# A Mamba block's front written out batch by batch, with its residual moved into the scan stage

## The chip, the cores and the metric

The kernel runs on one core of one Trainium2 chip. The metric is the time of one launch on the device in microseconds (us): the median of several runs. All data is float32 unless a tile is said to be something else.

## The reference, cut to what matters

The input is x, 8 batches of 512 tokens of 128 features. Four blocks follow each other, each added to its input: a Mamba block, a mixture of experts, an attention block, the same mixture of experts again. The change touches the Mamba block alone:

```
xl    = layernorm(x)                                  # (x - mean) * rstd
xn    = xl * rsqrt(mean(xl * xl) + eps) * norm_w
x_s,z = split(xn @ in_proj_w.T)                       # 256 channels each
u     = silu(causal_conv4(x_s) + conv_b)
dt,B,C= split(u @ x_proj_w.T)                         # 8, 16, 16
delta = softplus(dt @ dt_proj_w.T + dt_proj_b)
h_t   = exp(delta * A) * h_(t-1) + delta * u * B_t    # 16 states per channel
y     = (sum over states of h_t * C_t + u * D) * silu(z)
x     = x + (y @ out_proj_w.T + xl)                   # xl is the block's own residual
```

The last line is x * (1 + rstd) - mean * rstd + y @ out_proj_w.T, and both kernels compute it in that form.

## The kernel before, in words

The program is written by hand for each engine, and engines meet at semaphores. `setup` loads x into the tile `x_tok` (128 tokens by 32 groups by 128 features; four groups are one batch) and computes `mean`, `rstd` and `r12` (the product of both scales) for every token. `mamba` then runs two stages with a barrier between them: `mamba_front` and `mamba_scan`. The rest of the launch (the experts, attention, the experts) is the same code in both kernels.

**The front** makes, for each of 8 batches, `delta`, `du` = delta * u, `u`, `zs` = silu(z) and the turned B (tile `b_T`), all but the last kept in the large tile `arena`, and stores the rows of C to memory. A batch takes this way through the engines:

- VectorE (DVE in the rows) makes the normalised rows `xn_tok` (`normed`, L422, four instructions of 128x128); TensorE (PE) turns them (`turn`, L348); ScalarE (ACT) copies them out (`x_out`, L534); PE projects to x_s (L366) and to z (L360).
- The convolution: ACT makes the first tap (L540), DVE the other three taps for two channel halves, six instructions (`conved`, L449, of which one input is in PSUM and one in SBUF). ACT applies silu (`u_out`, L547; `gates` for z, L553).
- PE projects u (`x_proj`, L374), ACT copies (`xd_out`, L564), PE projects dt (L383). ACT takes the absolute value (L570), loads another function table, and makes exp and ln (`logs`, L575 and L578).
- softplus is max(v, 0) + log1p(exp(-|v|)), and log1p is made exact in pieces: DVE `lows` (L477, an SBUF tile to an SBUF tile, 1024 elements a partition); GpSimd (POOL) subtracts and adds (L606, L609); DVE `bounds` (L482) takes the minimum; DVE `deltas` (L461, two instructions, from PSUM) makes max(v, 0); POOL adds the two (L612, delta) and multiplies by u (L616, du). L471 on DVE copies the turned B.
- The residual: DVE multiplies `x_tok` by 1 + rstd and subtracts mean * rstd (`residual`, L436, four instructions of 128x128, SBUF to SBUF).

The order on each engine is the written order. For DVE, after a start written out for batches 0 and 1, a loop of B - 2 = 6 turns (L492 to L501) does in turn b: `normed(b + 2)`, `conved(b + 1)`, `lows(b)`, `deltas_and_b(b)`, `residual(b + 2)`, `bounds(b)`. PE, ACT and POOL have loops that fit this one. In POOL's loop a batch's four operations stand together: subtract, add, delta, du. For the last batch DVE itself does those operations (L511 to L518). A loop's turn computes addresses in registers, and each engine gives an increment more after some waits (`k.passed`).

**The scan stage** has 8 batches of 16 states, that is 128 steps. In a step ACT scales du by B (L722, four instructions) and makes exp(delta * A) (`d_a`, L730, two instructions), PE turns the product into PSUM (L820, or L817 for four of the states), DVE scans (L936), POOL multiplies by C (L681), PE adds up (L837). Each batch's output is made during the next batch's steps: in step 5 and 6 the gated rows are turned and copied (L953), in step 7 PE runs `project` (L856: for four groups of tokens two matmuls with `w_out` each) and DVE runs `add` (L949: one instruction over 512 elements, PSUM and x_tok into x_tok). In step 8 and 9 DVE makes the statistics of the next block's layernorm (L1069, L1074) and copies the next batch's du (L957), and in step 10 ACT makes the scale of these statistics (L1142) between its own scaling and its exps. At the start of the stage PE turns du of batch 0 into two banks (L794), ACT copies them (L708), and only then can ACT begin with L722.

## Time and profile before

| what | value |
|---|---|
| median of 3 runs | 1303.31 us (1302.11 to 1303.85) |
| the profiled execution, its own time | 1301.48 us |
| its span in the trace | 1299.7 us |
| front, first instruction of DVE to the end of its last | 24.20 to 150.90 us |
| scan stage begins | 152.03 us |
| TensorE busy, share of the span | 1067.4 us, 82% |
| VectorE | 928.6 us, 71% |
| ScalarE | 869.2 us, 67% |
| GpSimd | 540.6 us, 42% |

The spans of the profile are of one execution, whose own time is 1.8 us more than its span and 1.83 us less than the median of the runs. The shares are means over stages of different kinds. In the front and in the scan stage the engines stand otherwise than over the whole: what a change there is worth is read from stretches of the trace.

### The profile page before, as it was taken

The numbers are of one execution on the slowest core, as the hardware profiler recorded it, in microseconds if no ns is written. First come the engines' busy times: TensorE is split into PE (matmuls) and PEld (weight loads), VectorE is DVE, ScalarE is ACT, GpSimd is POOL, SyncE is SP. The second block draws the span as 40 slices with busy tenths as digits, with TensorE's granted clock in tenths as the row PEclk, the third lists the DMA queues.
The fourth block names the chain that finished last, engine by engine and source line by source line (L and its number), as shares of the span: only waits on it lengthen the run. The fifth ranks groups of instructions, "written<-read, shape, count | busy, mean of one in ns | idle before, by whom it ended". The sixth has DMA issues, their size and how long they took to land. (4 is left out here: it accounts for less than half of the span.)

```text
span 1299.7 us, 25092 instructions
## 1 busy us (share of the span) xinstructions
PE 1067.4 (82%) x7486; PEld 753.5 (58%) x7486; DVE 928.6 (71%) x2003; ACT 869.2 (67%) x1835; POOL 540.6 (42%) x367
## 2 busy tenths in 40 slices
PE   1677499988989888638966999999999999981797
PEld 1333278878878788518963454545454544541796
DVE  5899499889889889435644677757685867763564
ACT  1777699999999999216743756656675666660574
POOL 0367488899999999713440001010101011011344
PEclk9888699999999999878987999998999999995899
DMA  3000133223463453113321000000000000001331
GB/s 87 2 3 2 34 96 95 96 87 109 149 192 107 149 161 107 40 54 93 93 68 58 1 2 18 1 18 1 17 1 18 1 17 13 5 17 54 88 92 46
DMA packets 50631, 74.40 MB, mean 57 GB/s; under 512 B 7351, under 2 KB 28604, under 8 KB 50528
## 3 DMA queue, kind: packets, MB, share of 16 engines
q1 hardware_dynamic: 41504, 51.09, 13.5%
q0 software_dynamic: 5568, 12.66, 2.7%
q10 hardware_dynamic: 3456, 9.46, 2.3%
q8 instruction: 41, 0.67, 0.2%
q14 instruction: 62, 0.51, 0.1%
HBM read 57.86 MB, written 16.24 MB: 57 GB/s over the span
## 5 line engine op out<-in xcount | busy, mean ns | idle before, releaser
L936 DVE TENSOR_TENSOR_SCAN h<-d_a,p_dbu 128x1024 f32<-128x1024 f32 x128 | 290.1, 2279 | 37.0 <-ACT d_a L730 30.9
L681 POOL TENSOR_TENSOR h<-h,c_rep 128x1024 f32<-128x1024 f32 x128 | 299.4, 2364 | 25.2 <-DVE h L936 23.8
L1859 ACT ACTIVATE at_probs<-at_scores,at_min 128x512 f32<-128x512 f32 x256 | 184.1, 722 | 135.9 <-DVE at_min L1969 87.5
L1969 DVE CUSTOM_DVE_ANT_0 at_scores<-at_p_scores,arena 128x512 f32<-128x512 f32 x256 | 174.4, 684 | 89.5 <-PE at_p_scores L1735 51.2
L1217 POOL TENSOR_SCALAR r_row<-r_row 128x4 f32<-128x4 f32 x16 | 3.7, 231 | 476.3 <-DVEq L1130 476.3
L730 ACT ACTIVATE d_a<-arena,a_exp 128x511 f32<-128x511 f32 x256 | 169.1, 708 | 0.6 <-DVE h L936 0.5
L1742 PEld LDWEIGHTS at_p_probs_T<-ident,at_probs 128*128 128x128 f32 x1024 | 112.7, 142 | 93.7 <-issue 71.1
L1742 PE MATMUL at_p_probs_T<-ident,at_probs 128*128 128x128 f32 x1024 | 159.1, 283 | 6.4 <-ACT at_probs L1859 6.0
L722 ACT ACTIVATE b_du_T<-arena,b_T 128x256 f32<-128x256 f32 x384 | 162.5, 494 | 0.1
L1735 PE MATMUL at_p_scores<-arena,at_q_T 64*128 64x512 f32 x512 | 157.7, 643 | 5.5 <-DVE at_min L1969 3.8
L837 PE MATMUL p_y_T<-ident,h 128*128 128x128 f32 x1024 | 135.0, 275 | 7.4 <-POOL h L681 7.3
L837 PEld LDWEIGHTS p_y_T<-ident,h 128*128 128x128 f32 x1024 | 116.9, 142 | 9.9 <-POOL h L681 9.9
L820 PE MATMUL p_dbu<-ident,b_du_T 128*128 128x128 f32 x768 | 113.9, 284 | 5.0 <-ACT b_du_T L722 3.5
L1978 DVE COPY at_probs_T<-at_p_probs_T 128x512 f32<-128x512 f32 x128 | 88.2, 689 | 24.7 <-PE at_p_probs_T L1742 24.5
L820 PEld LDWEIGHTS p_dbu<-ident,b_du_T 128*128 128x128 f32 x768 | 86.5, 143 | 21.5 <-ACT b_du_T L722 9.1
L1827 ACT ACTIVATE at_probs_T<-at_p_probs_T 128x512 f32<-128x512 f32 x128 | 75.3, 588 | 26.6 <-PE at_p_probs_T L1742 24.1
L1416 PE MATMUL f_p_y<-f_w_cur,f_h_T 128*128 128x128 f32 x624 | 84.1, 278 | 7.0 <-issue 3.9
L1439 ACT ACTIVATE f_h_T<-f_p_h,f_w_cur 128x128 f32<-128x128 f32 x312 | 88.8, 376 | 1.4 <-PE f_p_h L1404 1.1
L1404 PE MATMUL f_p_h<-f_xg_T,f_w_cur 128*128 128x128 f32 x624 | 87.5, 286 | 0.9 <-issue 0.5
L1431 ACT ACTIVATE f_xg_T<-f_p_xg 128x128 f32<-128x128 f32 x78 | 21.7, 279 | 98.4 <-PE f_p_xg L1397 72.3
L1416 PEld LDWEIGHTS f_p_y<-f_w_cur,f_h_T 128*128 128x128 f32 x624 | 76.6, 193 | 8.9 <-issue 7.5
L1763 PE MATMUL at_p_o_T<-at_probs_T,arena 128*32 128x256 f32 x1024 | 80.0, 397 | 0.7 <-issue 0.7
(223 smaller groups left out, 1692.8 us busy)
## 6 DMA issues: line engine op xcount, KB each, us to landing
c_rep<-c_rows SPq DMA_DIRECT2D x128, 256.0 KB, 3.3
f_row<-expert_rows SPq DMA_DIRECT2D x78, 129.0 KB
arena<-in_w_all ACTq DMA_DIRECT2D x8, 578.0 KB
arena<-bias_by_distance ACTq DMA_DIRECT2D x8, 448.0 KB
x_tok<-in_x SPq DMA_DIRECT2D x4, 512.0 KB, 5.4
x_tok<-x_between SPq DMA_DIRECT2D x8, 256.0 KB, 2.8
expert_rows<-f_pad SPq DMA_DIRECT2D x10, 129.0 KB, 2.7
expert_rows<-f_pad ACTq DMA_DIRECT2D x8, 129.0 KB, 2.8
```

The lines of the kernel that those rows point to most:

```text
L681: nc.gpsimd.tensor_tensor(h[:, n % HS, :, :], h[:, n % HS, :, :], cc, ALU.mult).then_inc(prod_done, 1)
L722: nc.scalar.activation(b_du[:, s % SR, j, 0:width], src, ACT.Copy, scale=bT[:, one(b), j, s:s + 1].squeeze(1)).then_inc(scaled, 1)
L730: nc.scalar.activation(da[:, s % 2, ch, 1:], delta[:, one(b), ch, 1:].squeeze(1), ACT.Exp, scale=a_exp[:, ch, s:s + 1]).then_inc(da_ready, 1)
L820: mm = nc.tensor.transpose(dst, b_du[:, s % SR, j, ch * P:(ch + 1) * P], k.ident[:])
L837: mm = nc.tensor.matmul(p_yT[:, j, ch * P:(ch + 1) * P], h[:, n % HS, ch, j * P:(j + 1) * P], k.ident[:], is_transpose=SUM_BY_TRANSPOSE, s ...
L936: nc.vector.tensor_tensor_scan(h[:, n % HS, :, :].rearrange("p c t -> p (c t)"), da[:, s % 2, :, :].rearrange("p c t -> p (c t)"), p_dbu[: ...
L1416: mm = nc.tensor.matmul(py[:, r % YR, 0:D], ht[:, r % R, f, :], w_cur[:, r % R, FF + f * D:FF + (f + 1) * D], start=f == 0, stop=f == FC - 1)
L1439: ins = nc.scalar.activation(ht[:, r % R, f, :], ph[:, r % R, f, :], ACT.Gelu, bias=w_cur[:, r % R, 2 * FF + f:2 * FF + f + 1])
L1735: nc.tensor.matmul(psc[:, n % SCB, :], qT[par][half, hd // 2, it * P:(it + 1) * P], kT[par][half, hd // 2, :], start=True, stop=True).then ...
L1742: mm = nc.tensor.transpose(ppt[:, s % 2, j * P:(j + 1) * P], pr[:, s % 2, j * P:(j + 1) * P], k.ident[:])
L1859: nc.scalar.activation(pr[:, s % 2, :], sc[:, s % 2, :], ACT.Exp, scale=-1.0, bias=mn[:, s % 2:s % 2 + 1]).then_inc(probs_ready, 1)
L1969: V.tensor_tensor_reduce(sc[:, s % 2, :], psc[:, s % SCB, :], band[:, hd, w0:w0 + T], 1.0, 3.0e38, ALU.add, ALU.min, mn[:, s % 2:s % 2 + 1 ...
```

## The change

In the front, the loops of all engines are written out. A helper `each` runs i from -3 to 7 and calls every part with its own batch i + ahead. That gives five kinds of turn: three in which the pipeline fills, the full ones, and those in which first the normalised rows and then the convolution have run out. On DVE a turn is now `normed(i+3)`, `conved(i+1)`, `positive(i)`, `bounds(i-1)`, `take_b(i)`, `lows(i)`; on POOL `delta_du(i-1)`, `log_sums(i)`. `bounds` writes to a tile of its own, `delta_pos` has two buffers. `residual` is gone from the front.

In the scan stage, DVE's `add` is now four instructions of 128x128 that compute x * (1 + rstd) + p_x, and PE's `project` has one more matmul for each of the four groups, which puts -mean * rstd into the same PSUM bank before the others: its stationary operand is the turned table of shifts (32 partitions by 128 tokens), its moving operand one column of the identity, repeated 128 times. At the stage's start DVE makes the two tables, PE turns one, and ACT copies it ahead of its copies of du. In both `project` and `through_d` nothing else changes in order.

```diff
@@ mamba_front, each engine's turns @@
+        def each(*parts):
+
+            for i in range(-3, B):
+                for ahead, part in parts:
+                    if 0 <= i + ahead < B:
+                        part(i + ahead)
...
@@ tensor @@
-            with pe.Fori(0, B - 2) as b:
-                turn(b + 2)
-                in_proj(b + 2, z=False)
-                x_proj(b + 1)
-                dt_proj(b + 1)
-                in_proj(b + 2, z=True)
+            each((0, dt_proj), (2, project_in), (1, x_proj), (3, turn))
...
@@ vector @@
-            def residual(b):
-                dve.wait_ge(xn_ready, b + 1)
-                chn.wait()
-                for j in range(TPB):
-
-                    g = b * TPB + j
-                    xg = k.x[:, one(g), :].squeeze(1)
-                    chn.step(nc.vector.tensor_scalar(xg, xg, rone[:, one(g)], mr[:, one(g)],
-                                                     ALU.mult, ALU.subtract))
...
             def lows(b):
                 dve.wait_ge(e_ready, b + 1)
-                dve.wait_ge(delta_done, 1 + b)
+                after(dve, log1p_ready, b)
                 nc.vector.tensor_scalar(low[:], ex[:], 1.0, 1.0, ALU.add, ALU.subtract).then_inc(low_ready, 1)
...
                 dve.wait_ge(log_sum_ready, b + 1)
-                nc.vector.tensor_tensor(lg[:], low[:], ex[:], ALU.min).then_inc(log1p_ready, 1)
-
-            normed(0)
-            residual(0)
-            conved(0)
-            normed(1)
-            residual(1)
-
-            def turn(b, conv_next=True, norm_next=True):
-                if norm_next:
-                    normed(b + 2)
-                if conv_next:
-                    conved(b + 1)
-                lows(b)
-                deltas_and_b(b)
-                if norm_next:
-                    residual(b + 2)
-                bounds(b)
-
-            with dve.Fori(0, B - 2) as b:
-                chn.begin(b, 11)
-                turn(b)
...
+                after(dve, delta_done, b)
+                nc.vector.tensor_tensor(lm[:], low[:], ex[:], ALU.min).then_inc(log1p_ready, 1)
+
+            each((3, normed), (1, conved), (0, positive), (-1, bounds), (0, take_b), (0, lows))
...
@@ scalar @@
-            with act.Fori(0, B - 2) as b:
-                first_tap(b + 1)
-                logs(b)
-                x_out(b + 2)
-                u_out(b + 1)
-                gates(b + 1)
-                xd_out(b + 1)
...
+            each((1, first_tap), (0, xd_out), (2, x_out), (1, gates), (0, absolute), (1, u_out), (0, logs))
...
@@ gpsimd @@
-            with pool.Fori(0, B - 1) as b:
...
+            each((-1, delta_du), (0, log_sums))
...
@@ mamba_scan @@
+            act.wait_ge(shift_turned, 1)
+            nc.scalar.activation(shiftT[:], p_yT[0:NT, 0, 0:P], ACT.Identity).then_inc(shiftT_ready, 1)
             for half, bank in enumerate((p_x, p_small)):
                 act.wait_ge(du_turned, half + 1)
...
             def project(b):
                 pe.wait_ge(gT_ready, NC * b + NC)
                 for j in range(TPB):
+                    g = b * TPB + j
+                    nc.tensor.matmul(p_x[:, j * P:(j + 1) * P], shiftT[:], k.ident[0:NT, g:g + 1].to_broadcast([NT, P]),
+                                     start=True, stop=False)
                     for ch in range(NC):
-                        mm = nc.tensor.matmul(p_x[:, j * P:(j + 1) * P], u[:, one(b), ch, j * P:(j + 1) * P].squeeze(1),
-                                              w_out[:, ch, :], start=ch == 0, stop=ch == NC - 1)
+                        mm = nc.tensor.matmul(p_x[:, j * P:(j + 1) * P], u[:, b, ch, j * P:(j + 1) * P],
+                                              w_out[:, ch, :], start=False, stop=ch == NC - 1)
...
             turn_du(0, 1, p_small)
+            pe.wait_ge(shift_ready, 1)
+            nc.tensor.transpose(p_yT[0:NT, 0, 0:P], shift[:], k.ident[:]).then_inc(shift_turned, 1)
             pe.wait_ge(diag_ready, 1)
+            pe.wait_ge(shiftT_ready, 1)
...
             def add(b):
                 dve.wait_ge(projected, b + 1)
-                xb = k.x[:, bass.ds(b * TPB, TPB), :].rearrange("p g d -> p (g d)")
-                nc.vector.tensor_tensor(xb, p_x[:], xb, ALU.add).then_inc(added, 1)
+                for j in range(TPB):
+                    g = b * TPB + j
+                    xg = k.x[:, g, :]
+                    nc.vector.scalar_tensor_tensor(out=xg, in0=xg, scalar=one_plus[:, g:g + 1],
+                                                   in1=p_x[:, j * P:(j + 1) * P], op0=ALU.mult,
+                                                   op1=ALU.add).then_inc(added, 1)
```

In the order of VectorE's instructions, this is a turn of the front before (the loop; rows of address work, which repeat, are left out):

```order
L422 TENSOR_SCALAR xn_tok<-x_tok,mean,r 128x128
...
L449 SCALAR_TENSOR_TENSOR conv<-p_xz,vec,conv 128x511
...
L449 SCALAR_TENSOR_TENSOR conv<-p_xz,vec,conv 128x509
L477 TENSOR_SCALAR delta_low<-delta_e 128x1024
...
L461 TENSOR_SCALAR delta_pos<-p_dt,vec 128x512
...
L471 COPY b_T<-p_xdbc 128x64
...
L436 TENSOR_SCALAR x_tok<-x_tok,one_plus_rstd,mean_rstd 128x128
L482 TENSOR_TENSOR delta_ln<-delta_low,delta_e 128x1024
```

And this is a full turn after the change, from the `bounds` of one turn to that of the next:

```order
L460 TENSOR_TENSOR delta_log1p<-delta_low,delta_e 128x1024
L446 COPY b_T<-p_xdbc 128x64
L452 TENSOR_SCALAR delta_low<-delta_e 128x1024
L414 TENSOR_SCALAR xn_tok<-x_tok,mean,r 128x128 x4
L428 SCALAR_TENSOR_TENSOR conv<-p_xz,vec,conv 128x511 x2
L428 SCALAR_TENSOR_TENSOR conv<-p_xz,vec,conv 128x510 x2
L428 SCALAR_TENSOR_TENSOR conv<-p_xz,vec,conv 128x509 x2
L441 TENSOR_SCALAR delta_pos<-p_dt,vec 128x512 x2
L460 TENSOR_TENSOR delta_log1p<-delta_low,delta_e 128x1024
```

`lows` (L477, now L452) stood behind the convolution and ahead of the residual; now it stands right behind `bounds` and ahead of the normalised rows (L414).

On GpSimd, the operations of the written-out front come in this order (before, the loop had them as L606, L609, L612, L616, with address work ahead of L612 and L616):

```order
L541 TENSOR_TENSOR delta_low<-delta_e,delta_low 128x1024
L544 TENSOR_TENSOR delta_low<-delta_low,delta_ln 128x1024
L532 TENSOR_TENSOR arena<-delta_log1p,delta_pos 128x1024
L535 TENSOR_TENSOR arena<-arena 128x1024
L541 TENSOR_TENSOR delta_low<-delta_e,delta_low 128x1024
```

The order of the four is the same; the address work between them is gone.

On TensorE, around `project` in the scan stage, after the change:

```order
L772 MATMUL p_y_T<-ident,h 128x128 x8
L791 MATMUL p_r_x<-ident,shift_T 128x128
L794 MATMUL p_r_x<-w_out,arena 128x128 x2
L791 MATMUL p_r_x<-ident,shift_T 128x128
L794 MATMUL p_r_x<-w_out,arena 128x128 x2
L791 MATMUL p_r_x<-ident,shift_T 128x128
L794 MATMUL p_r_x<-w_out,arena 128x128 x2
```

Before, `L856 MATMUL p_r_x<-w_out,arena 128x128 x8` stood there alone; the four L791 are new, and the step's next products (L820 before, L755 now) come behind them.

## Rows read from the trace of the kernel before

**Rows 1.** Busy time by engine: a stretch of the front, and one of the scan stage.
```profile
core 0: us, PE busy (x) PEld busy (x) DVE busy (x) ACT busy (x) POOL busy (x), PEclk, DMA share, GB/s
104.00:118.20 14.20, 10.87 (x28) 5.32 (x28) 14.20 (x20) 10.49 (x15) 9.52 (x4) 0.82 0.01 2
450.00:500.00 50.00, 44.16 (x378) 40.87 (x376) 45.12 (x49) 48.17 (x109) 47.54 (x27) 1.00 0.51 154
```

**Rows 2.** Timeline of VectorE, one turn: start, duration, engine, line, operation, tiles.
```profile
103.90 0.67 DVE L477 TENSOR_SCALAR delta_low<-delta_e 128x1024 f32<-128x1024 f32 x1
104.50 1.39 DVE L461 TENSOR_SCALAR delta_pos<-p_dt,vec 128x512 f32<-128x512 f32 x2
105.95 4.07 DVE L436 TENSOR_SCALAR x_tok<-x_tok,one_plus_rstd,mean_rstd  x4
109.95 1.21 DVE L482 TENSOR_TENSOR delta_ln<-delta_low,delta_e 128x1024 f32<-128x1024 f32 x1
111.08 3.14 DVE L422 TENSOR_SCALAR xn_tok<-x_tok,mean,r 128x128 f32 x4
114.15 4.01 DVE L449 SCALAR_TENSOR_TENSOR conv<-p_xz,vec,conv 128x511 f32<-128x511 f32 x6
118.09 0.68 DVE L477 TENSOR_SCALAR delta_low<-delta_e 128x1024 f32<-128x1024 f32 x1
```

**Rows 3.** Timeline of GpSimd in the same turn.
```profile
104.66 2.35 POOL L606 TENSOR_TENSOR delta_low<-delta_e,delta_low 128x1024 f32<-128x1024 f32 x1 [2.21 <-DVE delta_low L477]
107.09 2.34 POOL L609 TENSOR_TENSOR delta_low<-delta_low,delta_ln 128x1024 f32<-128x1024 f32 x1
111.43 2.46 POOL L612 TENSOR_TENSOR arena<-delta_ln,delta_pos 128x1024 f32 x1 [2.00 <-DVE delta_ln L482]
114.27 2.36 POOL L616 TENSOR_TENSOR arena<-arena  x1 [0.38 <-POOL arena L612]
```

**Rows 4.** Single durations in ns by line: least, median, most; first and last start.
```profile
L436 DVE TENSOR_SCALAR x_tok<-x_tok,one_plus_rstd,mean_rstd x32: 333/343/2511, 25.5 to 123.9; - x24, 128x128 f32<-128x128 f32 x8
L477 DVE TENSOR_SCALAR delta_low<-delta_e x8: 672/676/1712, 47.0 to 142.3; 128x1024 f32<-128x1024 f32 x8
L461 DVE TENSOR_SCALAR delta_pos<-p_dt,vec x16: 730/734/743, 47.6 to 143.9; 128x512 f32<-128x512 f32 x16
```

**Rows 5.** Timeline of VectorE: the front's start, first batch, last loop batch and end.
```profile
24.39 1.10 DVE L422 TENSOR_SCALAR xn_tok<-x_tok,mean,r 128x128 f32<-128x128 f32 x4
46.97 0.69 DVE L477 TENSOR_SCALAR delta_low<-delta_e 128x1024 f32<-128x1024 f32 x1 [0.62 <-ACT delta_e L575]
53.04 1.21 DVE L482 TENSOR_TENSOR delta_ln<-delta_low,delta_e 128x1024 f32<-128x1024 f32 x1
136.16 1.23 DVE L482 TENSOR_TENSOR delta_ln<-delta_low,delta_e 128x1024 f32<-128x1024 f32 x1 [3.44 <-POOL delta_low L609]
149.67 1.23 DVE L518 TENSOR_TENSOR arena<-arena 128x1024 f32<-128x1024 f32 x1
```

**Rows 6.** Timeline of ScalarE at the scan stage's start.
```profile
154.20 0.59 ACT L708 ACTIVATE arena<-p_r_small 128x512 f32<-128x512 f32 x1
154.91 1.70 ACT L722 ACTIVATE b_du_T<-arena,b_T 128x256 f32<-128x256 f32 x4
```

**Rows 7.** Timeline in the scan stage around `project` and `add` of one batch.
```profile
267.49 2.05 PE L856 MATMUL p_r_x<-w_out,arena 128*128 128x128 f32 x16 [0.37 <-DVE arena L953]
269.38 1.04 PE L820 MATMUL p_dbu<-ident,b_du_T 128*128 128x128 f32 x8
269.58 0.69 DVE L949 TENSOR_TENSOR x_tok<-p_r_x,x_tok 128x512 f32<-128x512 f32 x1
270.51 2.29 DVE L936 TENSOR_TENSOR_SCAN h<-d_a,p_dbu 128x1024 f32<-128x1024 f32 x1 [0.24 <-PE p_dbu L820]
274.01 0.30 ACT L1142 ACTIVATE r_lnv<-r_mv,r_eps 128x4 f32<-128x4 f32 x1 [0.93 <-issue]
```

**Rows 8.** Timeline of TensorE: `project` of the last batch.
```profile
542.69 3.60 PE L856 MATMUL p_r_x<-w_out,arena 128*128 128x128 f32 x16 [0.78 <-DVE arena L953]
```

More of the change, by code:

```diff
@@ L346, in turn @@
                 pe.wait_ge(xn_ready, b + 1)
+                after(pe, xnT_ready, b)
                 for j in range(TPB):
@@ new lines, in project_z, with project_in @@
+            def project_z(b):
+                pe.wait_ge(xnT_ready, b + 1)
+                after(pe, z_taken, b * NC)
+                for j in range(TPB):
+                    at = j % 2 * DI
+                    mm = nc.tensor.matmul(pz[:, NC + j // 2, at:at + DI], xnT[:, j * P:(j + 1) * P], w_in[:, DI:],
+                                          start=True, stop=True)
+                    if j % 2:
+                        mm.then_inc(z_half_ready, 1)
+            def project_in(b):
+                if b == 0:
+                    project_x(b)
+                    project_z(b)
+                else:
+                    project_z(b)
+                    project_x(b)
@@ L369, in x_proj @@
             def x_proj(b):
-                pe.wait_ge(xd_ready, 1 + b)
-                pe.wait_ge(bT_ready, 1 + b)
+                after(pe, xd_ready, b)
+                after(pe, bT_ready, b)
                 for ch in range(NC):
                     pe.wait_ge(u_ready, b * NC + ch + 1)
-                    mm = nc.tensor.matmul(pxd[:], w_x[:, ch, :], u[:, one(b), ch, :].squeeze(1),
-                                          start=ch == 0, stop=ch == NC - 1)
+                    mm = nc.tensor.matmul(pxd[:], w_x[:, ch, :], u[:, b, ch, :], start=ch == 0, stop=ch == NC - 1)
@@ L455, in conved, with positive, take_b @@
                             ins.then_inc(conv_ready, 1)
-            def deltas(b, ch):
-                dve.wait_ge(delta_done, 1 + b)
-                dve.wait_ge(abs_ready, 1 + b * NC + ch + 1)
-                nc.vector.tensor_scalar(mpos[:, ch, :], pdt[:, ch, :], dt_b(ch), 0.0,
-                                        ALU.add, ALU.max).then_inc(pos_ready, 1)
-            def deltas_and_b(b):
-                deltas(b, 0)
-                deltas(b, 1)
+            def positive(b):
+                after(dve, delta_done, b - 1)
+                for ch in range(NC):
+                    dve.wait_ge(abs_ready, b * NC + ch + 1)
+                    nc.vector.tensor_scalar(mpos[:, b % 2, ch, :], pdt[:, ch, :], dt_b(ch), 0.0,
+                                            ALU.add, ALU.max).then_inc(pos_ready, 1)
+            def take_b(b):
                 dve.wait_ge(b_turned, b + 1)
-                k.passed(dve)
-                nc.vector.tensor_copy(bT[:, one(b), :, :].squeeze(1).rearrange("p j s -> p (j s)"),
+                nc.vector.tensor_copy(bT[:, b, :, :].rearrange("p j s -> p (j s)"),
                                       pxd[:, 0:TPB * NS]).then_inc(bT_ready, 1)
@@ L513, in _ @@
             chn.link(nc.vector.tensor_tensor(low[:], low[:], lg[:], ALU.add))
             chn.link(nc.vector.tensor_tensor(lg[:], low[:], ex[:], ALU.min))
-            dve.wait_ge(pos_ready, 1 + B * NC)
-            chn.link(nc.vector.tensor_tensor(delta[:, last, :, :], lg[:], mpos[:], ALU.add))
+            dve.wait_ge(pos_ready, B * NC)
+            chn.link(nc.vector.tensor_tensor(delta[:, last, :, :], lg[:], mpos[:, last % 2, :, :], ALU.add))
             dve.wait_ge(u_ready, B * NC)
             chn.link(nc.vector.tensor_tensor(du[:, last, :, :], delta[:, last, :, :], u[:, last, :, :], ALU.mult))
-            chn.wait()
@@ L593, in _, with delta_du @@
-            first_tap(B - 1)
-            logs(B - 2)
-            u_out(B - 1)
-            gates(B - 1)
-            xd_out(B - 1)
-            logs(B - 1)
+            each((1, first_tap), (0, xd_out), (2, x_out), (1, gates), (0, absolute), (1, u_out), (0, logs))
         @block.gpsimd
         def _(pool):
-            k.from_one(pool, delta_done)
-            with pool.Fori(0, B - 1) as b:
-                db = delta[:, one(b), :, :].squeeze(1)
-                pool.wait_ge(low_ready, b + 2)
+            def delta_du(b):
+                pool.wait_ge(log1p_ready, b + 1)
+                pool.wait_ge(pos_ready, b * NC + NC)
+                nc.gpsimd.tensor_tensor(delta[:, b, :, :], lm[:], mpos[:, b % 2, :, :], ALU.add).then_inc(delta_done, 1)
+                pool.wait_ge(delta_done, b + 1)
+                pool.wait_ge(u_ready, b * NC + NC)
+                nc.gpsimd.tensor_tensor(du[:, b, :, :], delta[:, b, :, :], u[:, b, :, :], ALU.mult).then_inc(du_done, 1)
```

177 lines of the change are left out of this document (68 added, 109 removed).

## The prediction

> **What bounds the kernel now.** I read the busy time by stretch first, then the timeline of one turn of the front on VectorE and on GpSimd, then the single durations of a few lines, and last the timeline of the scan stage around `project`. The front bounds itself on VectorE: of a stretch of 14.20 us it is busy for 14.20, TensorE for 10.87, ScalarE for 10.49, GpSimd for 9.52 [rows 1]. The turn's length stands in the starts of `lows`, 103.90 and 118.09: 14.19 us [rows 2]. But VectorE is not at work in all of it. The four residual instructions take 4.07 us and the four normalised rows 3.14 [rows 2], while four of the same form take 1.10 at the front's start, where GpSimd does nothing [rows 5]. The difference is held time. A residual instruction has a median of 343 ns and a most of 2511 [rows 4], and the long ones end with a GpSimd operation: the stretch of L436, 105.95 to 110.02, is the rest of L606 (until 107.01), all of L609 (107.09 to 109.43), and two free instructions [rows 2, 3]. So a VectorE instruction that goes from SBUF to SBUF in this form waits until the running GpSimd operation ends; in the gap of 0.08 us between two of them exactly one gets through. `deltas`, which reads PSUM, runs beside L606 with no hold (730 to 743 ns) [rows 3, 4], and so does the convolution beside L616.
>
> In the scan stage ScalarE is busy 48.17 of 50 us [rows 1]. Of the idle rest one piece recurs: in step 10 it waits 0.93 us for VectorE's statistics before L1142 [rows 7]. From step 7 to there the path is PE and VectorE: `project` ends at 269.54, PE's next products L820 at 270.42, and VectorE's scan waits 0.24 for them, with `add` done at 270.27, just before [rows 7]. A delay there reaches ScalarE, which has nothing to make it up with.
>
> **The change, part by part.**
>
> *The full turn of the front.* The residual's 4.07 us go. That alone would leave 10.1 us of VectorE, but the order decides who is held. Now `lows` follows `bounds` at once, so GpSimd gets all its four operations in one row: delta and du of batch i-1, subtract and add of batch i. The normalised rows stand right behind `lows`, so they meet these operations: one gets through at each boundary, and the last at about the end of the add. Only then come the convolution, max(v, 0) and `bounds`, which nothing overlaps on GpSimd. From one `bounds` to the next:
> - `bounds` 1.13 (109.95 to 111.08) [rows 2], and about 0.1 until GpSimd starts;
> - GpSimd's 2.35 + 2.35 + 2.35 + 2.34, with three gaps of 0.08: 9.63 [rows 3] (L612 and L616 at the plain 2.35, since their 0.38 of gap goes with the address work);
> - `lows`: it is issued while delta runs, held, and then keeps GpSimd's du off. Its own 0.68 less the overlap is 0.55;
> - the last normalised row 0.26 ((1.10 - 0.33) / 3) [rows 4, 5], the convolution 3.94 (114.15 to 118.09), max(v, 0) 1.32 (1.39 less 0.07 of overlap) [rows 2].
>
> Together 16.9 us, against 14.2. Between bounds 0 and bounds 3 there are three such turns. In the next three the normalised rows have run out; the convolution then lies beside GpSimd, which becomes the bound: 1.21 + 0.1 + 9.63 + 0.55 = 11.5. Six turns: 3 x 16.9 + 3 x 11.5 = 85.2, against 83.1 (53.04 to 136.16) [rows 5]: **+2.1**.
>
> *The fill.* VectorE now makes three batches of rows before the first convolution, and the third waits until PE has turned the second, behind both projections; PE puts both projections of batch 1 ahead of `x_proj(0)`, and ScalarE puts `gates` and `u_out` of batch 1 ahead of the first exp. I put the convolution of batch 0 3.2 us later and the rest of the chain to `lows(0)` even, so that starts at 50.2 instead of 46.97 [rows 5]. From there to the first `bounds`: 0.68 + 0.08 + 2.35 + 0.08 + 2.34 (held rows), 0.6 for the last two, 3.94 + 1.32: 11.4, against 6.07 now [rows 2, 3, 5]. Fill: 3.2 + 5.3 = **+8.5**. I am least sure of the 3.2: from 0 (PE and ScalarE have slack while the pipeline fills) to 5.
>
> *The end.* From the last `bounds` to the front's end there are 14.7 us now (136.16 to 150.90) [rows 5]. After: 1.2 + 0.1 + 2.35 (delta) + 0.55 (`lows`) + 2.35 (du) + five closing operations at 1.25 = 12.8, **-1.9**. This takes it that the first closing operation, which reads two SBUF tiles, is held by du. No such operation stands beside a running GpSimd one in the trace: the bounds are 0 (L461, not held) and 2.35 (L477, held up to 1712 ns) [rows 4]. I take the upper, since its sources are both in SBUF like L477's. The Trainium skill (page "SBUF — State Buffer", section "Who interferes with whom") says that a tensor_tensor with both inputs in SBUF contends with GpSimd's reads; by it the sum stays, without it it would be about 2 lower. No run here shows it yet. The two small tables leave the front: -0.2.
>
> Front: 2.1 + 8.5 - 1.9 - 0.2 = **+8.5**.
>
> *The scan stage's start.* ScalarE's copies of du now wait behind PE's third transpose and the table's copy. Its second copy starts at 154.20, and the first scaling at 154.91 [rows 6]; what comes between PE's second group and the first copy now is a small transpose and a small copy, some 0.25 each, two hand-overs, and the first copy itself that moves behind them: **+0.8** (0.3 to 1.2).
>
> *Each batch's project and add.* Four more matmuls of 128 columns. Eight take 16 records in 2.05 us, with the next products 1.89 after the start [rows 7], so four cost 0.95 (the least would be half, if a matmul of 32 rows were cheaper; no row shows that). `add` becomes four of 128x128, for which I take the 1.10 of rows 5 (the bounds are the 0.69 that one takes now and four at L449's 0.67). PE: products end 0.95 later. VectorE: add starts at 270.5, ends at 271.6, and the scan starts there, against 270.51: 1.15. Nothing between there and ScalarE's wait in step 10 makes it up. Seven batches: 7 x 1.15 = **+8.0**. The last batch's project runs at 3.60 / 16 = 0.225 a record [rows 8], with VectorE waiting for it: 8 x 0.21 + 0.4 = **+2.1**.
>
> **Sum:** 8.5 + 0.8 + 8.0 + 2.1 = 19.4 us. The profiled execution would be 1301.5 + 19.4 = 1320.9, the median, 1.8 above it, 1303.3 + 19.4 = **1322.7**.
>
> **The rivals.**
> - *The scan's additions lie in ScalarE's shadow.* For it: VectorE is busy 45 of 50 us, so it has slack somewhere; against it: the 0.24 and 0.93 of rows 7 are on the very path. Then only the last batch's 2.1 and the start's 0.8 remain: 1303.3 + 11.4 = 1314.7. Chance 0.12.
> - *More rows get through a boundary.* For it: at L616's gap of 0.38 a free instruction did get through; if the gaps stay wide, the rows are done by the end of the subtract, and each held turn is 2.4 shorter, the fill too: 1322.7 - 4 x 2.4 = 1313.1. Against it: the gap without address work is 0.08 [rows 3]. Chance 0.12.
> - *Faster: the rows are not held at all in the new order*, because VectorE comes first to what the two share, or because the hold belonged to the residual's write of x_tok. Then GpSimd's 11.0 (11.5 less the 0.55) bounds every turn. `bounds(0)` would come at 50.2 + 7.0 (VectorE's own work) = 57.2, the last at 123.2, the end some 9.3 later at 132.5: the front ends 18.4 earlier, and the launch takes 1303.3 - 18.4 + 10.9 = 1295.8. It decides once the rows of a turn take under 1.5 us. Against it: xn_tok itself took 3.14 in rows 2. Chance 0.08.
> - *Longer still:* TensorE's granted clock, 0.82 of full in a turn now [rows 1], falls with longer idle stretches and stretches the fill's chain: up to 1330. Chance 0.06.
>
> The forecast keeps 0.62. **The range** is 1310 to 1330: it takes in the first two rivals, the fill's 0 to 5 and the closing hold, and leaves out the third. About 0.2% (2.6 us) is what a measurement of this kernel can tell from no change. Faster by more than that 0.08, within it 0.04, slower 0.88.
>
> **What would show it.** In the profile after: L414 with 24 of its rows near 0.34 us or less and some ten of over 2; a full turn of 16.9 and late ones of 11.5 by the starts of L460; GpSimd's four operations back to back; the first L460 near 61 or 62; L791 as 8 records a batch; `add` of some 1.1 us and VectorE's next scan 1.15 later than project allows now; ScalarE's wait before its step 10 scale near 2.1. I am wrong if the rows L414 take about 1.1 a batch in full turns, or if the stretch from project to L1142 keeps its length of 6.5 us (267.49 to 274.01) [rows 7].

## The result, and the profile after

The changed kernel takes 1321.13 us (median of 4 runs, 1319.66 to 1322.63), the kernel before 1303.58 on the same chip. The ratio is 1.0137, with an interval of 1.0113 to 1.0161: slower by 17.5 us, where 1322.7 was forecast. The profiled execution took 1321.48 us, with a span of 1319.5 against 1299.7. Busy time hardly moves: TensorE 1086.8 us against 1067.4, VectorE 926.7 against 928.6.

The place of the time comes from the same instructions in both traces. "How much later" is the start after less the start before.

| instruction | before | after | later by |
|---|---|---|---|
| `lows(0)` | 46.97 | 52.68 | 5.71 |
| first `bounds` | 53.04 | 64.00 | 10.96 |
| last closing operation of the front | 149.67 | 158.82 | 9.15 |
| scan of batch 0, step 1 | 162.07 | 171.72 | 9.65 |
| scan of batch 3, step 0 | 295.25 | 307.23 | 11.98 |
| scan of batch 7, step 0 | 483.23 | 501.26 | 18.03 |
| scan of batch 7, step 15 | 527.95 | 547.18 | 19.23 |
| last `r_dest` of the scan stage | 562.37 | 583.39 | 21.02 |

(`r_dest`, the table of each token's place in the next block, is made once a batch; the last one ends the scan stage's own work.) Behind the scan stage 1.2 us come back (the span is 19.8 longer), but that is scatter: the stretch from the last `r_dest` to the end, whose code is the same everywhere, takes 734.9 to 739.1 us in all kernels here but one. So the loss lies in the front (9 us) and in the scan stage (12 us).

**The front.** First VectorE, then GpSimd, in one full turn: start, duration, engine, line, operation. Rows 2 and 3 show the same turn before.

```profile
64.00 1.21 DVE L460 TENSOR_TENSOR delta_log1p<-delta_low,delta_e 128x1024 f32<-128x1024 f32 x1
66.39 1.81 DVE L452 TENSOR_SCALAR delta_low<-delta_e 128x1024 f32<-128x1024 f32 x1 [1.05 <-ACT delta_e L519]
68.12 7.35 DVE L414 TENSOR_SCALAR xn_tok<-x_tok,mean,r 128x128 f32<-128x128 f32 x4
75.39 4.02 DVE L428 SCALAR_TENSOR_TENSOR conv<-p_xz,vec,conv 128x511 f32<-128x511 f32 x6
79.33 1.40 DVE L441 TENSOR_SCALAR delta_pos<-p_dt,vec 128x512 f32<-128x512 f32 x2
80.65 1.21 DVE L460 TENSOR_TENSOR delta_log1p<-delta_low,delta_e 128x1024 f32<-128x1024 f32 x1
```

```profile
65.29 2.36 POOL L532 TENSOR_TENSOR arena<-delta_log1p,delta_pos 128x1024 f32<-128x1024 f32 x1 [7.06 <-DVE delta_log1p L460]
67.72 2.68 POOL L535 TENSOR_TENSOR arena<-arena 128x1024 f32<-128x1024 f32 x1
70.37 2.34 POOL L541 TENSOR_TENSOR delta_low<-delta_e,delta_low 128x1024 f32<-128x1024 f32 x1
72.78 2.35 POOL L544 TENSOR_TENSOR delta_low<-delta_low,delta_ln 128x1024 f32<-128x1024 f32 x1
```

The turn is 16.65 us (64.00 to 80.65) against 14.19 [rows 2]. Four normalised rows last 7.35 us, from the middle of du to the end of the add; the convolution begins at 75.39, when GpSimd is through (75.13) and does nothing for the rest of the turn. Of the 32 rows 21 take 0.33 to 0.35 us, and 11 take 1.74 to 2.51.

**The scan stage**, around `project` and `add` of one batch (rows 7 of before): TensorE, VectorE, ScalarE.

```profile
279.50 0.48 PE L791 MATMUL p_r_x<-ident,shift_T 32*128 32x128 f32 x2 [0.37 <-DVE arena L903]
279.91 0.71 PE L794 MATMUL p_r_x<-w_out,arena 128*128 128x128 f32 x4
280.56 0.48 PE L791 MATMUL p_r_x<-ident,shift_T 32*128 32x128 f32 x2
...
283.08 0.71 PE L794 MATMUL p_r_x<-w_out,arena 128*128 128x128 f32 x4
283.63 1.04 PE L755 MATMUL p_dbu<-ident,b_du_T 128*128 128x128 f32 x8
```

```profile
279.36 2.28 DVE L882 TENSOR_TENSOR_SCAN h<-d_a,p_dbu 128x1024 f32<-128x1024 f32 x1
283.83 1.12 DVE L897 SCALAR_TENSOR_TENSOR x_tok<-x_tok,one_plus_rstd,p_r_x 128x128 f32<-128x128 f32 x4 [2.19 <-PE p_r_x L794]
284.87 2.28 DVE L882 TENSOR_TENSOR_SCAN h<-d_a,p_dbu 128x1024 f32<-128x1024 f32 x1
```

```profile
284.70 1.71 ACT L657 ACTIVATE b_du_T<-arena,b_T 128x256 f32<-128x256 f32 x4 [1.22 <-PE p_dbu L755]
288.36 0.30 ACT L1092 ACTIVATE r_lnv<-r_mv,r_eps 128x4 f32<-128x4 f32 x1 [1.95 <-DVE r_mv L1024]
299.66 0.58 ACT L1098 ACTIVATE arena<-p_r_x 128x512 f32<-128x512 f32 x1
```

`project` takes 4.29 us (279.50 to 283.79), not 2.05. VectorE waits 2.19 for it, and its scans of steps 7 and 8 start 5.51 us apart. ScalarE's wait in step 10 has grown from 0.93 to 1.95. But L1098 in step 13 waits for nothing, where the same copy in the trace of before waited 1.17 us (0.83 in later batches):

```profile
286.57 0.60 ACT L1148 ACTIVATE arena<-p_r_x 128x512 f32<-128x512 f32 x1 [1.17 <-PE p_r_x L1168]
```

So a batch loses in step 7 and gets a part back in steps 13 to 15. Taken over whole batches (scan 0 to scan 0 of the next), after is 2.35 us longer than before in batch 1, where nothing comes back, no longer in batch 2, 1.84 in batch 3 and 1.4 in batches 4 to 6. The experiments take both places apart.

### The profile page after: what moved, and what is told of

Same layout as the page of the kernel before. It is cut to its first block and busy times, and to the rows that moved or that the text cites. A ratio compares the mean times of both kernels' runs of the same rounds, so it can differ in the third digit from the quotient of the medians.

```text
span 1319.5 us, 24770 instructions
## 1 busy us (share of the span) xinstructions
PE 1086.8 (82%) x7551; PEld 763.4 (58%) x7551; DVE 926.7 (70%) x1995; ACT 868.4 (66%) x1835; POOL 542.6 (41%) x367
## 5 line engine op out<-in xcount | busy, mean ns | idle before, releaser
L755 PE MATMUL p_dbu<-ident,b_du_T 128*128 128x128 f32 x768 | 118.7, 284 | 6.4 <-ACT b_du_T L657 4.0
L755 PEld LDWEIGHTS p_dbu<-ident,b_du_T 128*128 128x128 f32 x768 | 84.0, 142 | 31.8 <-ACT b_du_T L657 14.1
```

What stands on the lines that cost most here:

```text
L755: mm = nc.tensor.transpose(dst, b_du[:, s % SR, j, ch * P:(ch + 1) * P], k.ident[:])
```

## The experiments

All times are medians, and ratios are to the kernel before, run beside each. Those medians of before lie between 1302.44 and 1305.58 us, so kernels of different sets are better compared by their ratios. "Step 7" is the distance of VectorE's scans 7 and 8 of a batch, "late" that from scan 13 to scan 0 of the next batch, both from VectorE's timeline; the trace of before has 3.16 and 10.2, that of after 5.50 and 9.04 (batches 3 to 6).

### The scan's additions apart

**scan_plain**: no shift matmul, the plain add, no tables.

```diff
-                    nc.tensor.matmul(p_x[:, j * P:(j + 1) * P], shiftT[:], k.ident[0:NT, g:g + 1].to_broadcast([NT, P]),
-                                     start=True, stop=False)
...
-                    nc.vector.scalar_tensor_tensor(out=xg, in0=xg, scalar=one_plus[:, g:g + 1],
-                                                   in1=p_x[:, j * P:(j + 1) * P], op0=ALU.mult,
...
+                nc.vector.tensor_tensor(xb, p_x[:], xb, ALU.add).then_inc(added, 1)
```

> The changed kernel with the scan stage as before: project without the shift matmuls, one plain add of 512 elements a batch, no tables. The residual's share of the normalised input is left out altogether, so the time is that of the front's change alone. Theory (front +9.1 us, the rest of the +17.5 from the scan's additions): 1309 to 1311 us. Rival (the additions lie in ScalarE's shadow and the front costs it all): 1318 to 1321.

**adds_only**: the first part of this diff alone (no shift matmuls), without the shift's table as well. **shift_only**: the other part alone (one plain add in place of the four).

> The changed kernel with the four adds but without the shift matmuls and their table (the term -mean*rstd is left out). Theory (a delay under the 1.2 us that the late steps regain costs nothing but in the last batch): within 1 us of scan_plain, about 1310.5. Rival (the adds' 0.43 us a batch adds up): 8 x 0.43 = 3.4 above scan_plain, 1313.5 to 1314.

> The changed kernel with the four shift matmuls a batch kept but the four adds back to one plain add (the factor 1 + rstd on the old row is left out). Theory (project's extra 2.2 us is what costs, and of each batch's delay about 1.2 us is regained in the late steps): 7 x (2.0 - 1.2) above scan_plain and about 2 for the last batch, 1317 to 1319. Rival (nothing is regained, the delays add up plainly): 7 x 2.0 + 2, 1325 or the changed kernel's own time; rival (the four adds are the cost): near scan_plain's 1310.

| kernel | us | ratio, interval | step 7 | late | last `r_dest` later than before |
|---|---|---|---|---|---|
| scan_plain | 1309.71 | 1.0040, 1.0021 to 1.0058 | 3.16 | 10.2 | 7.73 |
| adds_only | 1310.81 | 1.0035, 1.0020 to 1.0050 | 3.27 | 10.1 to 10.2 | 8.97 |
| shift_only | 1326.45 | 1.0161, 1.0129 to 1.0192 | 5.39 | 9.04 | 19.09 |
| after | 1321.13 | 1.0137, 1.0113 to 1.0161 | 5.50 | 9.04 | 21.02 |

scan_plain's ratio puts the front's change at 2.7 to 7.6 us, where its trace has 7.7 by the last `r_dest` and 9.1 by the first scans; the profiled execution of before is one of the faster ones. The four adds cost nothing that a run can tell: their 0.43 us (1.12 less 0.69) lie beside TensorE's products, and step 7 grows by 0.11. From scan 0,1 (batch 0, step 1) to scan 7,15 adds_only takes 365.79 us and scan_plain 365.78. The shift matmuls are 2.23 us of step 7, 1.2 of which the late steps return from batch 3 on. They can't return more than that: at 9.04 ScalarE waits for nothing in them. In batch 1 they are at 9.04 in the kernel before too, and return nothing. So the rival "lies in the shadow" held for the adds and fell for the matmuls.

shift_only was expected at 1317 to 1319 and took 1326.45. Its theory had the scan stage 7.6 us longer than scan_plain's; by the last `r_dest` it is 11.4 (581.46 less 570.10), of which 8.7 lie between scan 0,1 and scan 7,15 where 5.6 were expected: batch 1 returned nothing. It is 1.9 us ahead of after there. The rest of its launch takes 740.8 us (1322.3 less 581.46) against 736.1. It leaves a factor out, so its later stages work on other values; but scan_plain leaves out more, and its rest takes 737.0. The cause of these 4 us is open.

### Why four small matmuls cost 2.2 us

**shift_wide** (one matmul of 512 columns ahead of the others) and **shift_first** (all four of 128 columns ahead, each with its weight load), each against after:

```diff
+                rows = k.ident[0:NT, b * TPB:(b + 1) * TPB].unsqueeze(2).to_broadcast([NT, TPB, P])
+                nc.tensor.matmul(p_x[:].rearrange("p (j i) -> p j i", i=P), shiftT[:], rows,
+                                 start=True, stop=False, skip_group_check=True)
```

```diff
                     nc.tensor.matmul(p_x[:, j * P:(j + 1) * P], shiftT[:], k.ident[0:NT, g:g + 1].to_broadcast([NT, P]),
-                                     start=True, stop=False)
+                                     start=j == 0, stop=False, skip_group_check=True)
+                for j in range(TPB):
                     for ch in range(NC):
```

> The changed kernel, computing the same, with one shift matmul of 512 columns ahead of the eight others in place of four of 128 between them. Theory (the cost is the change between 32-row and 128-row matmuls, some 0.3 us a time): project takes 2.9 to 3.1 us in place of 4.29, each batch gains 1.2, the time is 1321 - 7 x 1.2 - 1 = 1311 to 1314. Rival (a column of a 32-row matmul is dear in itself, 0.56 us for 128): project stays at 4.2 to 4.4 and the time within 2 us of the changed kernel's.

> The changed kernel, computing the same, with the four shift matmuls of 128 columns together ahead of the eight others, each with its own weight load. It parts two readings of shift_wide. Theory (a change between 32-row and 128-row matmuls is what is dear): project 3.0 to 3.3 us, VectorE's step from scan 7 to scan 8 at 4.3 to 4.6 us, 1313 to 1316 us. Rival (each separate matmul of 32 rows with its own weight load is dear, wherever it stands): project 4.1 to 4.3, the step 5.4 to 5.5, 1319 to 1322.

TensorE in shift_wide, and then in shift_first:

```profile
277.50 1.12 PE L790 MATMUL p_r_x<-ident,shift_T 32*128 32x512 f32 x2 [0.37 <-DVE arena L904]
278.56 2.05 PE L794 MATMUL p_r_x<-w_out,arena 128*128 128x128 f32 x16
```

```profile
277.92 1.15 PE L791 MATMUL p_r_x<-ident,shift_T 32*128 32x128 f32 x8 [0.37 <-DVE arena L905]
279.00 2.05 PE L795 MATMUL p_r_x<-w_out,arena 128*128 128x128 f32 x16
```

Both have the same work as after and take 3.1 us for `project` in place of 4.29. Step 7 is 4.32 and 4.35, late 9.1; the times are 1314.88 (ratio 1.0065, 1.0040 to 1.0089) and 1315.17 (1.0091, 1.0067 to 1.0115). shift_wide is just above the 1311 to 1314 expected, shift_first within its range. Separate weight loads are not it (1.15 against 1.12). What is dear is that matmuls of 32 rows and of 128 rows (32*128 and 128*128 in the lines) alternate: (4.29 less 3.13) / 4, about 0.3 us a group. Grouping leaves one change of kind where after has seven, so a change costs (4.29 less 3.13) / 6, about 0.19 us. The weight loads (PEld) in after's `project` show where:

```profile
279.50 0.29 PEld L791 LDWEIGHTS p_r_x<-ident,shift_T 32*128 32x128 f32 x2 [0.61 <-DVE arena L903]
279.91 0.52 PEld L794 LDWEIGHTS p_r_x<-w_out,arena 128*128 128x128 f32 x4
```

Behind a change the load starts together with its matmul (279.91 both), 0.20 us after the start of the matmul before, and the second matmul 0.21 after the first. Within a kind the load starts 0.11 ahead of its matmul, and matmuls follow each other at 0.11.

Is it the number of rows, or that the small matmul's moving operand is one column repeated? The trace of before answers, since attention changes between 64 and 128 rows with ordinary operands:

```profile
709.41 1.04 PE L1742 MATMUL at_p_probs_T<-ident,at_probs 128*128 128x128 f32 x8
710.37 1.13 PE L1735 MATMUL at_p_scores<-arena,at_q_T 64*128 64x512 f32 x4
```

At such a change, 91 times in this trace, the first 64-row matmul starts 0.20 us after the last 128-row one, while the 128-row ones follow each other at 0.11. So the repeated column isn't needed, and the delay at a change could be read before the prediction.
The Trainium skill (page "TensorE: Matmul & The Clock Gate", section "LDWEIGHTS (loading the stationary operand)") says that a 32x128 load takes as long as a 128x128 one. The trace agrees: a load of 32 rows takes 0.18 to 0.19 us, one of 128 rows 0.19. By that rule the four cost what four large ones do; grouped they cost about that (0.27 each, against 0.24 for a w_out matmul), but alternating they cost 0.56, of which the rule says nothing.

### The order of the front

**rows_late** moves the rows in VectorE's turn; **rows_act** leaves the place and gives them to ScalarE.

```diff
-            each((3, normed), (1, conved), (0, positive), (-1, bounds), (0, take_b), (0, lows))
+            each((1, conved), (0, positive), (3, normed), (-1, bounds), (0, take_b), (0, lows))
```

```diff
+                    ins = nc.scalar.activation(xn[:, j, :], k.x[:, g, :], ACT.Identity, scale=k.r12[:, g:g + 1],
+                                               bias=nmr[:, g:g + 1])
...
-            each((1, first_tap), (0, xd_out), (2, x_out), (1, gates), (0, absolute), (1, u_out), (0, logs))
+            each((3, normed), (1, first_tap), (0, xd_out), (2, x_out), (1, gates), (0, absolute), (1, u_out), (0, logs))
```

> The changed kernel with the normalised rows of a turn behind the convolution and max(v, 0), just ahead of bounds. Theory (the rows are dear because GpSimd's four operations run behind bounds and lows, and a row gets through only between two): they take 1.1 to 1.5 us, a full turn some 12.3 us in place of 16.65, three turns 13 less, and the fill 4 to 9 less: 1299 to 1305 us. Rival (the order in VectorE's turn doesn't matter, the turn is bound by the chain through TensorE and ScalarE): a full turn stays over 15.5 and the time above 1317.

> The changed kernel with the normalised rows made on ScalarE (scale r12, bias -mean*r12) at the start of its turn; VectorE's order is the same less the rows. Theory (the hold is on VectorE alone): no row takes over 0.4 us, a full turn comes to 11.2 to 12.5 us, the last convolution no longer waits for GpSimd, 1298 to 1304 us. Rival (any engine's read of x beside GpSimd is held, or ScalarE's four more operations bound the turn): rows of 1 us and more or a turn over 14, 1310 or more.

rows_late, VectorE's turn:

```profile
70.63 1.21 DVE L460 TENSOR_TENSOR delta_log1p<-delta_low,delta_e 128x1024 f32<-128x1024 f32 x1
...
74.79 4.04 DVE L428 SCALAR_TENSOR_TENSOR conv<-p_xz,vec,conv 128x511 f32<-128x511 f32 x6
79.57 1.41 DVE L441 TENSOR_SCALAR delta_pos<-p_dt,vec 128x512 f32<-128x512 f32 x2 [0.74 <-ACT delta_abs L512]
80.89 1.77 DVE L414 TENSOR_SCALAR xn_tok<-x_tok,mean,r 128x128 f32<-128x128 f32 x4
82.59 1.21 DVE L460 TENSOR_TENSOR delta_log1p<-delta_low,delta_e 128x1024 f32<-128x1024 f32 x1
```

One line moved, a full turn of 11.96 us in place of 16.65, and 1302.28 us (ratio 0.9995, 0.9977 to 1.0013). The time is in the 1299 to 1305 expected, though four rows take 1.77 us and not 1.1 to 1.5. The front's last operation starts at 139.41, 19.4 earlier than after's. The convolution, which isn't held (0.73 to 0.75 us an instruction, as in after and before), now lies beside GpSimd's operations, and the rows meet only the end of the last one. The first `bounds` comes at 58.68, 5.3 earlier, 2.5 of it for the held rows behind `lows(0)`, and 2.8 because `lows(0)` comes at 49.87 and not 52.68.

These 2.8 us are of two kinds. After and the five kernels of the two sections above have the same front, and their `lows(0)` lies between 51.70 and 52.72. TensorE's granted clock from 34 to 44 us is 0.83 in after and 1.00 in shift_wide, whose `lows(0)` is at 51.70, and 1.00 in rows_late too. So 1.0 us goes by the clock and 1.8 is the rows' place. VectorE at the second convolution, in after and then in rows_late:

```profile
44.56 1.11 DVE L414 TENSOR_SCALAR xn_tok<-x_tok,mean,r 128x128 f32<-128x128 f32 x4 [5.74 <-PE p_xT L355]
45.59 4.02 DVE L428 SCALAR_TENSOR_TENSOR conv<-p_xz,vec,conv 128x511 f32<-128x511 f32 x6
```

```profile
41.37 4.17 DVE L428 SCALAR_TENSOR_TENSOR conv<-p_xz,vec,conv 128x511 f32<-128x511 f32 x6 [4.67 <-ACT conv L488]
```

In after the fourth batch of rows stands ahead of the second convolution and waits for TensorE's `turn` (L355), which stands behind `x_proj(0)`. ScalarE's `u_out(1)` waits for that convolution, and the first exp stands behind `u_out(1)`. The third batch of rows ahead of the first convolution moves that by 4 us (34.80 in after, 35.27 in shift_wide, 30.60 in rows_late), but `x_proj(0)` comes at 41.23 in shift_wide and 41.15 in rows_late all the same.

In rows_act no row is held: the 32 take 477 to 493 ns, those beside GpSimd's operations too. But ScalarE had no room:

```profile
78.92 4.04 DVE L424 SCALAR_TENSOR_TENSOR conv<-p_xz,vec,conv 128x511 f32<-128x511 f32 x6 [2.95 <-ACT conv L493]
85.01 1.21 DVE L456 TENSOR_TENSOR delta_log1p<-delta_low,delta_e 128x1024 f32<-128x1024 f32 x1
```

```profile
76.57 1.65 ACT L479 ACTIVATE xn_tok<-x_tok,minus_mean_r,r 128x128 f32<-128x128 f32 x4 [1.02 <-PE p_xT L357]
78.12 1.42 ACT L493 ACTIVATE conv<-p_xz,vec 128x512 f32<-128x512 f32 x2
```

The rows wait there for TensorE and push the first tap back, on which VectorE now waits 2.95. A turn is 13.25 (71.76 to 85.01), the first `bounds` 7.8 later than in after, and the time 1320.78 (ratio 1.0129, 1.0093 to 1.0166), not the 1298 to 1304 expected. ScalarE's rows aren't held, but the place was wrong again.

**logs_first**, on rows_late: for batch 0 only, ScalarE does exp and ln ahead of gates and u of batch 1.

```diff
+                if i == 0:
+                    behind = ((0, absolute), (0, logs), (1, gates), (1, u_out))
```

> rows_late with one turn of ScalarE's order changed: the exp and ln of batch 0 ahead of the gates and u of batch 1. Theory (the fill's later lows(0) is ScalarE's order: gates and u of batch 1, 2.24 us, stand ahead of the first exp): the exp starts some 2.2 earlier, lows(0) at 48.2 to 48.6 where VectorE's own order then holds it, in place of 49.87. Rival (the exp waits for TensorE's dt): lows(0) stays within 0.3 of 49.87. The launch's time moves by less than 2 us either way.

`lows(0)` stays at 49.65, as the rival says, since the exp waited for TensorE's dt. But this run doesn't clear ScalarE's order: its granted clock from 34 to 44 us is 0.83, against 1.00 in rows_late, and `x_proj(0)` comes 0.82 later (41.97 against 41.15). From there the exp starts 6.59 us on, against 7.63 in rows_late, so the order is worth about 1.0 us, which the clock hides. The launch moved by far more than expected: the gates of batch 1 came at 52.01, the projection behind them at 53.24, and the first `bounds` at 66.22 in place of 58.68. 1312.73 us (1.0059, 1.0039 to 1.0079); 3.6 us of it are two falls of the clock in `project` (the last section). So of the 2.9 us by which rows_late's `lows(0)` is later than before's, about 1.0 is ScalarE's order, by this reading. The rest stands with TensorE, which starts `x_proj(0)` at 41.15 in rows_late and at 36.81 before; a kernel with TensorE's old order was not run.

**fold_loop**: the kernel before, its loop less the residual, with the scan's part of the change.

```diff
-                if norm_next:
-                    residual(b + 2)
```

> The kernel before with the scan's part of the change alone: the front's loop as before less its residual, the shift matmuls and the four adds in the scan stage. Theory (in the old order bounds follows GpSimd's subtract and add, which start with lows, so the residual's 4.07 us lay almost wholly beside them): a full turn goes from 14.19 to 13.6 or 13.8 us, the front ends 2 to 4 earlier, the scan's additions cost some 11.5: 1311 to 1314 us. Rival (the 4.07 us come off each turn): a turn of 10.1 to 10.6, 1303.5 - 24 + 11.5 = 1291.

VectorE, one turn:

```profile
108.06 1.23 DVE L467 TENSOR_TENSOR delta_ln<-delta_low,delta_e 128x1024 f32<-128x1024 f32 x1 [3.43 <-POOL delta_low L590]
109.20 3.14 DVE L417 TENSOR_SCALAR xn_tok<-x_tok,mean,r 128x128 f32 x4
...
121.77 1.22 DVE L467 TENSOR_TENSOR delta_ln<-delta_low,delta_e 128x1024 f32<-128x1024 f32 x1 [3.43 <-POOL delta_low L590]
```

A turn of 13.71, with 3.43 us of waiting where the residual stood: its 4.07 us were worth 0.5. 1314.41 us (1.0067, 1.0038 to 1.0095), just above the 1311 to 1314 expected; two falls of the clock in `project` make its scan stage some 3.4 us longer than after's. The last `bounds` of the loop comes 2.4 earlier than before (133.79 against 136.16), but the front's last operation only 0.8, less than the 2 to 4 expected. So the fold had next to nothing to gain in the old order.

### Versions that beat both

**best1**: rows_late's order, the residual on ScalarE in the front, the scan stage as before. **best2**: rows_late with shift_wide. **best3**: rows_late's order, the scan stage as before, the residual on VectorE where it idles beside an idle GpSimd, and the first normalised rows no longer behind the wait for the weights. Its residual:

```diff
+            def residual_in_fill(b):
+                if b < 3:
+                    residual(b)
...
+            for g in range(3 * TPB, NT):
+                chn.step(nc.vector.tensor_scalar(k.x[:, g, :], k.x[:, g, :], one_plus[:, g:g + 1], mr[:, g:g + 1],
+                                                 ALU.mult, ALU.subtract))
```

> Meant to beat both kernels: the changed kernel's written-out front with the normalised rows just ahead of bounds, the residual done in the front by ScalarE (scale 1 + rstd, bias -mean*rstd, four operations at the end of its turn), and the scan stage as before with one plain add. Theory: scan as before, so 1310.5 less the 17 to 22 of the new order, 1289 to 1295 us. Rival (ScalarE becomes the front's bound): a full turn over 13.5, 1297 or more; rival (the order doesn't matter): 1308 or more.

> rows_late with shift_wide's project: the normalised rows ahead of bounds, one shift matmul of 512 columns, the four adds. Theory (the two parts add up, -19 and -6): 1294 to 1298 us. Rival (an earlier scan stage meets something else): above 1300.

> rows_late's order with the scan stage's project and add as before. The residual is VectorE's again, but only where it idles and GpSimd does nothing: batches 0 to 2 behind their normalised rows in the fill, the 20 rows of batches 3 to 7 while the scan stage waits for its first scan (an idle of 4.95 us in rows_late, 20 rows at 0.26 are 5.2). The first normalised rows no longer wait for the weights. Theory: rows_late less the scan's 11 to 13: 1287 to 1292 us. Rival (the 20 rows are held there, or the stage's start is not idle): each held row 2.3, 1295 or more.

best1: 1297.62 us (0.9955, 0.9936 to 0.9974), above the 1289 to 1295 expected; its turns are 12.8 us, since ScalarE's 1.63 us of residual delay the first tap as in rows_act. best2: 1296.12 (0.9925, 0.9901 to 0.9949); the two parts add up. best3: **1292.15** (0.9906, 0.9873 to 0.9939), 29 us below after and 12 below before. VectorE in best3 at the scan stage's start:

```profile
142.62 5.21 DVE L883 TENSOR_SCALAR x_tok<-x_tok,one_plus_rstd,mean_rstd 128x128 f32<-128x128 f32 x20
147.75 2.28 DVE L892 TENSOR_TENSOR_SCAN h<-d_a,p_dbu 128x1024 f32<-128x1024 f32 x1
151.16 2.29 DVE L892 TENSOR_TENSOR_SCAN h<-d_a,p_dbu 128x1024 f32<-128x1024 f32 x1 [1.14 <-PE p_dbu L766]
```

Twenty residual rows take 0.26 us each, and none is held. They end some 0.8 us after the first scan could have started (ScalarE's `d_a` is done at 146.93). That costs nothing, since the second scan waits 1.14 us for TensorE all the same.

## Why the prediction was right, and where it erred

- **The hold.** Right. Three rows of a full turn take 1.74 to 2.51 us and the fourth 0.33. The hold was said to be on the form and the place; rows_late and rows_act show both. The faster rival (rows not held) fell, and so did "more rows get through a boundary": one does at each. The rival of a falling clock fell for the turns: the granted clock is 0.96 in the full turn from 64.00 to 80.65, and was 0.82 in a turn before.
- **The turns.** 16.9 forecast, 16.65 measured; the late ones 11.5 and 11.2 (125.15 to 136.35). From first to last `bounds` there are 83.52 us against 83.12, so +0.4, not +2.1.
- **The fill** was mis-sized. "The convolution of batch 0 3.2 us later and the rest of the chain even": `lows(0)` came 5.71 later, outside the 0 to 5 given. The 11.4 from there to the first `bounds` was 11.32. So the fill cost 10.96, not 8.5. The convolution ended 3.6 us later (38.83 against 35.23), near the 3.2, but by rows_late that hardly moves `x_proj(0)`; it is "the rest of the chain even" that failed. Of the 5.71, 1.8 are the rows ahead of the second convolution (rows_late), and about 1.0 is ScalarE's order (logs_first). Another 1.0 goes with the clock from 34 to 44 us, which is 0.83 in after and 1.00 in shift_wide; but it is 0.83 in the trace of before too, so this part can't be put down to the change. The other 1.9 are left for TensorE's order, which no run parts.
- **The end.** 12.8 forecast, 12.53 measured (147.52 to 160.05). The unseen hold of the first closing operation was the upper bound's: 3.24 us against 1.23 for the next. The Trainium skill's rule (page "SBUF — State Buffer", section "Who interferes with whom") on operations with both inputs in SBUF agrees with these rows:

```profile
151.76 3.24 DVE L465 TENSOR_TENSOR delta_low<-delta_e,delta_low 128x1024 f32<-128x1024 f32 x1
155.04 1.23 DVE L467 TENSOR_TENSOR delta_low<-delta_low,delta_ln 128x1024 f32<-128x1024 f32 x1
```

```profile
151.25 2.67 POOL L535 TENSOR_TENSOR arena<-arena 128x1024 f32<-128x1024 f32 x1
```

- **The scan stage's start.** +0.8 forecast, about 0.6 measured (9.65 less the 9.07 by which the stage begins later).
- **Each batch.** Near in sum, by two errors that cancel. "Four cost 0.95" took the price of a `w_out` matmul with no price for a change of kind, but alternating they cost 2.24, so step 7 is 2.35 longer and not 1.15. "Nothing between there and ScalarE's wait in step 10 makes it up" was true as far as it looked; steps 13 to 15 make up 1.2, because ScalarE's wait for TensorE before L1148 goes. Net it is 1.5 a batch in batches 3 to 6 (18.03 less 11.98, over four), with 0.2 to 0.3 from elsewhere. In batch 1 it is 2.35, with nothing made up, and in batch 2 nothing. Together 9.6 us from scan 0,1 to scan 7,15, against the 8.0 forecast.
- **The last batch.** `project` began at 561.00 and the first add at 568.60, 7.60 us against 3.63 (542.69 to 546.32): 4.0 more, where 1.7 was forecast for it. It is the same mis-sized step at a lower clock: the granted clock is 0.50 over all of these 7.60 us, the level of 1.2 GHz, and there the alternation costs more. This stretch takes 7.60 in each kernel that alternates, 5.82 in shift_wide and shift_first, and 3.49 to 3.82 with no shift matmul. What reached the last `r_dest` was 1.8 (19.23 to 21.02), against 2.1 for the term, and that is luck. `project` itself began only 18.31 later, 0.9 less than scan 7,15. Behind the add, TensorE's next eight turns (L1487) take 3.17 us, while before they (L1537) took 4.87, 1.7 more. Neither was in the forecast.

The front's +8.5 (9.15 measured), the start's +0.8 and the scan's +10.1 were each within 1.5 us, but inside them errors of 2.5 (fill), 1.7 (turns) and twice 1.2 (step 7 and its return) cancel. The direction and the mechanisms of the front were foreseen; that the total came within 1.6 us of the measured one is in part luck.

## What to carry to other kernels

Before taking work off an engine, look whether the next instruction there waits for another engine anyway: 4.07 us of residual were worth 0.5. Place instructions that go from SBUF to SBUF on VectorE (of the forms that were held here) where GpSimd rests, and put those that read PSUM beside its work; this one line was worth 19 us. Keep TensorE's small matmuls of fewer rows together, and not between those of 128 rows. After a delay, follow the whole period, and not only to the next wait: slack further on gives a bounded part back, here 1.2 us in a late batch and none in batch 1. Before a shift of a microsecond or less is put down to an edit, compare the granted clock of the stretch in both traces.

## What was not expected of the hardware

- Matmuls of 32 rows alternating with 128-row ones cost 0.56 us each, grouped 0.27, since each change of kind costs about 0.19.
- TensorE's clock can fall in the midst of the alternating `project`. Two of seven did so in fold_loop and two in logs_first, none in the profiles of the other kernels, those that alternate (after, rows_late, rows_act, shift_only) among them. Two stretches of fold_loop, each around one `project`, by the view of windows; PEclk is the granted clock. Then TensorE's rows within the first:

```profile
core 0: us, PE busy (x) PEld busy (x) DVE busy (x) ACT busy (x) POOL busy (x), PEclk, DMA share, GB/s
269.60:277.00 7.40, 7.25 (x34) 6.21 (x35) 3.41 (x6) 4.19 (x10) 5.51 (x6) 0.69 0.35 105
317.90:325.30 7.40, 7.03 (x52) 5.94 (x50) 5.21 (x7) 6.22 (x13) 5.48 (x5) 1.00 0.37 118
```

```profile
271.22 0.71 PE L846 MATMUL p_r_x<-w_out,arena 128*128 128x128 f32 x4
272.27 1.06 PE L846 MATMUL p_r_x<-w_out,arena 128*128 128x128 f32 x4
273.98 1.22 PE L846 MATMUL p_r_x<-w_out,arena 128*128 128x128 f32 x4
```

The same four matmuls go from 0.71 to 1.22 us, from the level of 2.4 GHz to that of 1.2 (the granted clock is 0.50 from 273.33 to 277.00), though TensorE is at work without a gap from 269.75 on; step 7 is 7.39 us in place of 5.50. What makes it fall was not settled.
